# Counting the edges of a graph: from scattered additions to one-hot products on the matrix engine

## The reference

```
e   = leaky_relu(alpha_s[src] + alpha_d[dst]);  a = exp(e - max over dst) / sum over dst
out = segment_sum(h[src] * a, dst)                      # layer 0
agg = segment_sum(norm * (h[row] + edge_fea), col)      # layer 1, five times
```

## Time and profile before

| | us |
|---|---|
| runs of the kernel before | 4120.7, 4135.0, 4138.2 (median 4135.0) |
| span of the profiled execution | 4111.2 |
| attention loop, from first to last zz | 249 to 1694 of the span |
| busy: PE, DVE, POOL, ACT | 3273, 2226, 2136, 1341 |

### The profile page before, as it was taken

How to read it: one execution, slowest core, us unless ns; L and a number is a source line. 1 busy time by engine, 2 the same in 40 slices (tenths; PEclk the granted TensorE clock), 3 DMA queues, 4 the chain that set the end, 5 groups by cost and what they waited for, 6 DMA issues and landing times. The chain is left out here.

```text
span 4111.2 us, 65888 instructions
## 1 busy us (share of the span) xinstructions
PE 3273.1 (80%) x17046; PEld 2215.9 (54%) x17047; DVE 2226.4 (54%) x7140; ACT 1340.9 (33%) x3098; POOL 2136.4 (52%) x1893
## 2 busy tenths in 40 slices
PE   0758888888887878769999999996976777777778
PEld 0446666666655555546555555554455555555544
DVE  5657777777777777772222222225244445554468
ACT  3123333333333333232213131314553333433322
POOL 4366777777788888544454636310004545554510
PEclk9878898888989898879999999997998888888889
DMA  7468656656665556334444545342943323332320
GB/s 302 64 172 261 140 142 145 141 141 145 138 140 133 139 135 138 64 83 133 156 144 141 172 126 170 124 130 52 263 119 93 91 85 96 94 94 87 90 55 21
DMA packets 472113, 530.37 MB, mean 129 GB/s; under 512 B 192361, under 2 KB 376791, under 8 KB 471925
## 3 DMA queue, kind: packets, MB, share of 16 engines
q0 software_dynamic: 142496, 237.86, 24.0%
q1 hardware_dynamic: 316808, 271.48, 22.5%
q10 hardware_dynamic: 12749, 20.33, 1.4%
HBM read 438.46 MB, written 70.54 MB: 124 GB/s over the span
## 5 line engine op out<-in xcount | busy, mean ns | idle before, releaser
L1136 PE MATMUL p_out<-rows,hot 128*128 128x266 f32 x2048 | 665.4, 454 | 68.2 <-DVE rows L1273 53.5
L2217 POOL DMA_INDIRECT col_rows<-col_dram,m_idx x440 | 417.6, 949 | 473.1 <-ACT m_idx L2297 333.3
L1061 POOL DMA_INDIRECT count_dram<-number,place x348 | 587.9, 1689 | 144.9 <-issue 107.7
L1053 POOL DMA_INDIRECT rows<-att_dram,idx x512 | 526.1, 1028 | 216.7 <-issue 143.0
L1705 POOL DMA_INDIRECT rec_dram<-records,edge_place x416 | 407.8, 980 | 429.6 <-PE p_hi L1738 200.6
L1634 PE MATMUL p_lo<-cbuf,parts 128*128 128x400 f16 x1750 | 583.4, 333 | 5.1 <-issue 5.1
L1635 PE MATMUL p_hi<-cbuf,parts 128*128 128x400 f16 x1750 | 583.4, 333 | 4.0 <-issue 4.0
L1136 PEld LDWEIGHTS p_out<-rows,hot 128*128 128x128 f32 x2048 | 409.8, 222 | 170.1 <-DVE rows L1273 85.2
L1144 PE MATMUL p_out<-mask,ident_bf 128*128 128x240 bf16 x1788 | 361.4, 287 | 1.7 <-issue 1.7
L1273 DVE TENSOR_TENSOR rows<-rows 128x512 f32<-128x512 f32 x512 | 349.8, 684 | 0.2 <-issue 0.2
L1662 DVE TENSOR_TENSOR node_sum<-p_hi,low_sb 128x400 f32<-128x400 f32 x80 | 46.0, 574 | 557.5 <-ACT low_sb L1653 491.6
(11 more groups left out here) (421 smaller groups left out, 6126.7 us busy)
## 6 DMA issues: line engine op xcount, KB each, us to landing
cbuf<-count_dram SPq DMA_DIRECT2D x40, 2500.0 KB
dl_rep<-dl_dram SPq DMA_DIRECT2D x128, 256.0 KB
count_dram<-zeros SPq DMA_DIRECT2D x20, 1000.0 KB
g_rows<-count_dram SPq DMA_DIRECT2D x25, 800.0 KB, 4.7
rec_dram<-blank ACTq DMA_DIRECT2D x1, 17600.0 KB
m_group_rows<-rec_dram SPq DMA_DIRECT2D x110, 160.0 KB
records<-in_edges POOLq DMA_DIRECT2D x32, 520.0 KB
key_rep<-key_dram SPq DMA_DIRECT2D x64, 256.0 KB
```

The source lines that it names most:

```text
L1053: nc.gpsimd.indirect_dma_start(rows[r][:, u, :], None, att_dram, bass.IndirectOffsetOnAxis(ap=idx[r][:, u:u + 1].bitcast(U32), axis=0)).th ...
L1061: nc.gpsimd.indirect_dma_start(count_dram, bass.IndirectOffsetOnAxis(ap=place[r][:, n, c:c + 1].bitcast(U32), axis=0), number[r][:, 2 * n ...
L1136: m = nc.tensor.matmul(p_out[q][:, side, 0:HALF], hot[k][:, u, :], rows[k][:, u, side * HALF:(side + 1) * HALF], start=(u == 0), stop=(u = ...
L2217: nc.gpsimd.indirect_dma_start(col_rows[q][:, u, :], None, col_dram, bass.IndirectOffsetOnAxis(ap=idx[q][:, u:u + 1].bitcast(U32), axis=0) ...
```

## The change

The counts are made by PE. Destinations are cut in blocks ("windows") of WD = 10 nodes; for each the plan makes one or more count steps: (chunk of 128 edges, window). There are CT = 768 of them, CS = 6 per group of the attention loop. For a count step DVE makes two one-hot tables in bf16, `lo_hot` (edge by source modulo 128) and `key_hot` (edge by 25 source tiles times 10 destinations, 250 columns; -1 steps of other chunks match nothing), and PE multiplies them into a PSUM area `counts` of 3 banks; the table `step_table` says which window of the area a step belongs to. ACT copies the six windows (128 x 1500) to a 16-bit area `taken`, that lies over `x_sb`, once per group; SP stores it once per round (240 columns of 3200 rows, pieces of 480 bytes). A window that a group leaves open is taken into the next by `carry`.

```
 DVE, per group                                              # removed: alike x2/x4, if_first, at_place
+def count_hots(g, q, first, last):
+    for v in range(first, last):
+        TS(lo_hot[q][:, v, :], iota_bf[:], column(lo_step, g * CS + v), None, ALU.is_equal)
+        one = TS(key_hot[q][:, v, :], iota_key[:], column(key_step, g * CS + v), None, ALU.is_equal)
 PE, per group                                               # removed: keep_clock x7 (14 products)
             if within(j, 1):
                 turn_back(j + 1)
                 node_tops(j + 1, (k + 1) % 4)
+            at = (*read_registers(... j * CS, 1 ...), *read_registers(... j * CS + 1, CS - 1 ...))
+            add_up(j, k, 0)
+            add_up(j, k, 1)
+            clear(j)              # waits evacuated >= j; 3 products of 512 columns, fp16
+            if not is_first(j):
+                carry(at[0])      # 1 product of 250 columns
+            pe.wait_ge(hots_ready, j + 1)
+            for v in range(CS // 2): count(q, v, at[v])       # 250 columns each, bf16
+            add_up(j, k, 2)
+            for v in range(CS // 2, CS): count(q, v, at[v])
             if within(j, 2): turn(j + 2)
             if within(j, 1): look_up(j + 1, tiles[k])
             add_up(j, k, U - 1)
 ACT, per group, behind Exp(j) and ahead of take_scores(j + 2)
+def evacuate(b, n, r):
+    act.wait_ge(counted, n)
+    (at,) = read_registers(... take_table ...)
+    nc.scalar.copy(taken[:, :, bass.ds(at, CS * WD)]..., counts[:]...).then_inc(evacuated, 1)
 SP, once per round
+    sp.wait_ge(evacuated, i * 4); sp.wait_ge(stored, i * 16)
+    sp.dma_start(count_dram...[:, :, bass.ds(to, WIDE)], taken[:, :, bass.ds(side, WIDE)])
 POOL, per group                                             # removed: pair() x1/x2, place_ready wait
                 for u in range(U): gather((k + 3) % 4, u)
```

More of the change, by code:

```diff
@@ L893, in rounds @@
                 work(GROUPS - 4 + k, k, GROUPS // 4 - 1)
-        def rounds_in_two(engine, work):
-            for k in range(4):
-                work(k, k, 0, True)
-            for first, last, late in ((1, LATE_ROUNDS, True), (LATE_ROUNDS, GROUPS // 4 - 1, False)):
-                with engine.Fori(first, last) as i:
-                    for k in range(4):
-                        work(i * 4 + k, k, i, late)
-            for k in range(4):
-                work(GROUPS - 4 + k, k, GROUPS // 4 - 1, False)
-        def issued(k, i, late):
-            return i * (BODY - 2) + (PRE + (0, 4, 6, 8)[k]) if late else i * BODY + (PRE + PARTS[k][0] - 2 * LATE_ROUNDS)
         def within(j, ahead):
@@ L1055, in gather, with work @@
                                 bass.IndirectOffsetOnAxis(ap=idx[r][:, u:u + 1].bitcast(U32), axis=0)).then_inc(rows_in[r], 16)
-                        def pair(r, n, before):
-                            pool.wait_ge(placed, before * 16)
-                            pool.nop().then_inc(waits_passed, 1)
-                            for c in range(2):
-                                nc.gpsimd.indirect_dma_start(
-                                    count_dram, bass.IndirectOffsetOnAxis(ap=place[r][:, n, c:c + 1].bitcast(U32), axis=0),
-                                    number[r][:, 2 * n + c:2 * n + c + 1], None, compute_op=ALU.add).then_inc(placed, 16)
-                        def work(j, k, i, late):
-                            ahead = within(j, 3)
-                            r, before = (k + 3) % 4, issued(k, i, late)
-                            second = k == 0 or (k == 2 and not late)
-                            pool.wait_ge(place_ready, j + 1)
-                            if k % 2 == 0:
-                                pair(k, 0, before)
-                            if ahead:
+                        def work(j, k, i):
+                            if within(j, 3):
                                 pool.wait_ge(idx_ready, j + 4)
@@ L1076, in work @@
                                 pool.nop().then_inc(waits_passed, 1)
[L1077 to L1088 removed]
+                                for u in range(U):
+                                    gather((k + 3) % 4, u)
+                        nc.gpsimd.memset(nothing[:], 0.0).then_inc(empty_ready, 1)
                         for g in range(3):
@@ L1139, in add_up, with clear @@
                                 m.then_inc(sums_ready, 1)
-                        def keep_clock(k, n, fresh=False):
-                            for i in range(n):
-                                nc.tensor.matmul(p_out[k % 2][:, i % 2, 272:], ident_bf[:], mask[:, 1, 0:240], start=fresh, stop=True,
-                                                 skip_group_check=True)
+                        def clear(j):
+                            pe.wait_ge(empty_ready, 1 if is_first(j) else 2)
+                            if not is_first(j):
+                                pe.wait_ge(evacuated, j)
+                            for v in range(CS * AT // HALVES):
+                                nc.tensor.matmul(counts[:, v * HALVES:(v + 1) * HALVES], ident16[:], nothing[:], start=True, stop=False,
+                                                 skip_group_check=True)
@@ L1147, in work @@
                         def work(j, k, tiles):
-                            if not (isinstance(j, int) and j < 2):
-                                pe.wait_ge(added, j - 1)
-                            keep_clock(k, 2, True)
+                            q = k % 2
                             if within(j, 1):
                                 turn_back(j + 1)
-                                keep_clock(k, 2)
                                 node_tops(j + 1, (k + 1) % 4)
-                            for u in range(U - 1):
-                                keep_clock(k, 2)
-                                add_up(j, k, u)
+                            table = step_table[:].rearrange("o b i -> o (b i)")
@@ L1158, in work @@
+                            add_up(j, k, 2)
+                            for v in range(CS // 2, CS):
+                                m = count(q, v, at[v])
+                            m.then_inc(counted, 1)
                             if within(j, 2):
```

445 lines of the change are left out of this document (232 added, 213 removed).

## The result

The changed kernel is slower: 4259.8 us (median of 4 runs, 4239.1 to 4269.7) against 4133.9 (4120.7 to 4138.2), a ratio of 1.030 with a 95% interval of 1.027 to 1.034. The prediction was 3938, with a range of 3845 to 4055.

The account below looks back on a forecast made before the run. POOL's scatters were taken to bound the loop, then PE's chain. Terms -22 - 9 + 5 - 178 + 10 + 4 - 1 = -191 us took the 4111.2 span to 3920, forecast 3938 us, range 3845 to 4055.

Parts of the forecast that it names:

- POOL's scatters: Attention loop before: POOL's queue of gathers and scatters makes rows late; the loop loses 1.9 us per group to scatters.
- The chain of 9.66 us: Attention loop: PE's dependent steps of one group at full clock, 9.66 us, above DVE's 9.2, set the period.
- the fourth rival: Attention loop: without the fillers PE's clock falls and the kernel gets slower than before; 4318 us at f = 0.5, chance 0.06.
- 9.95 + 6 f: Loop period in us if a share f of groups runs at 1.2 GHz, where about 6 us of PE stream double.
- the floor: Loop period of 9.95 us per group: PE's chain of 9.66 plus 0.3 for DVE's table read.
- PE's register reads: Behind `node_tops`, six table values in two calls per group: taken at 0, at most 2.4 us.
- evacuation hidden: Attention loop: ACT's copy of 1500 columns, 1.9 us behind Exp, ends before PE reaches `clear`, so it costs nothing.
- single p_out free: Attention loop: `add_up(j, 0)` waiting for DVE to have added the previous sums costs nothing.
- third rival: Attention loop: stores of 480-byte pieces hold the DMA engines at 10.6 to 11.7 us a group; 4020 to 4160 us, chance 0.12.
- Ahead of the loop: Before the last barrier: no zero fill, early chunks or key work, less the new selection block; -26 at best, net -22 us.
- The barrier's -9: Last barrier ahead of the loop: without POOL's early scatters DVE goes on 9 us earlier.
- Behind the loop: After the last group: last evacuation and store +4 us (0 to 10), late scatters -1, reload of x hidden.

Follow-up runs that it names:

- e2: The kernel before with its 14 filler products per group left out (`keep_clock` returns at once); time +0.2%, period 11.12 us, clock 0.74.
- e7: The changed kernel with 14 fillers, constant places and the late three count products moved behind look_up; ratio moved within its interval against fillers and constants alone.
- e11: The changed kernel with 6 fillers in PE's waits, split early place reads and late counts behind look_up; 4034.6 us against 4113.6 before, ratio 0.980.
- e1: The changed kernel with the 14 filler products per group back at their old places; period 11.35 us, clock 0.96, 0.8% slower than before.
- e5: The changed kernel run again, unedited; 3967.4 us against 3827.2 before, period 12.22 us, clock 0.78.
- e3: The changed kernel with PE's count places as constants instead of register reads (wrong columns); loop 1427 us first to last zz, clock 0.81.
- e6: The changed kernel with 14 fillers and constant places together; loop 1349 us first to last zz, ratio to before 0.984.
- e18: e15 with PE's and DVE's node tiles also constants instead of table reads (sums land in wrong tiles); mean period 9.74 us.
- e15: The changed kernel with 6 fillers, late counts, constant places and small stores (one tile of 25); mean period 10.25 us.
- e14: e11 with constant places, so PE reads no register inside a group; mean period 10.40 us.
- e9: e8 with each store of the count matrix cut to one tile of 25 (128 pieces instead of 3200); period 10.61 us.
- e10: The changed kernel with 14 fillers, late counts behind look_up and one group's places read before the round's store; ratio to before 0.992.
- e12: The kernel before run again, unedited, beside the variants; 1440 us of loop, first zz at 248.8 us.
- e16: e8 run again, side by side with e17; period 11.27 us.
- e17: The small-store version e9 run again, side by side with e16; period 10.62 us.
- e4: The changed kernel with PE's two register reads moved ahead of the next group's turning product; ratio to before 1.029.
- e8: The changed kernel with 14 fillers, real places read ahead of the turning product and late counts behind look_up; period 11.66 us.
- e13: e11 with one group's places read behind the node products instead of the turning product; no gain that can be measured.

## Why the prediction was wrong

**What bounds before (POOL's scatters): right.** e2 makes PE slower (clock 0.74) at nearly the same time (+0.2%), and ACT waits for gathered rows as before.

**The chain of 9.66 us: the pieces were right at full clock.** In e7, at 0.99 and with no reads, a plain group gives

```profile
884.63 0.27 DVE L1321 TENSOR_TENSOR zz<-p_node,rows 128x64 f32<-128x64 f32 x1 [0.68 <-PE p_node L1145]
...
888.24 0.16 DVE L1258 TENSOR_SCALAR absent<-p_node 128x4 f32<-128x4 f32 x1
...
890.12 1.17 PE L1154 MATMUL p_out<-rows,hot 128*128 128x266 f32 x4 [0.40 <-DVE rows L1300]
...
894.73 0.26 DVE L1321 TENSOR_TENSOR zz<-p_node,rows 128x64 f32<-128x64 f32 x1 [0.28 <-PE p_node L1145]
```

3.61 + 1.88 + 4.61 against 3.27 + 1.93 + 4.46. The third piece of e7 has four fillers more and three count products less than the one predicted. The 1.49 us for 3286 new columns hold: in the kernel after, clear, carry and three counts take 1.09 us (1029.87 to 1030.96) and the other three 0.32. With 6 fillers (e11) the plain groups take 9.5. In the kernel after the same three pieces are 3.15 + 2.81 + 5.24 = 11.2: the second holds the read and a slow add_up 0, the third a slow add_up 1.

**The step that failed: the chain was taken "at full clock".** The prediction saw that "keepers ran while PE waited; most of the new products stand on the chain", and counted this as columns only. It is also what kept the clock. This was the fourth rival, at a chance of 0.06; its formula, 9.95 + 6 f with f = (1 - 0.77) / 0.5 = 0.46, gives 12.7 where 12.4 came. That it comes so close is luck: it puts 2.8 us on the clock and nothing on the reads. In the plain group above the eight slow products cost 8 x 0.22 = 1.8 us, and the fillers give back 0.87 us a group (e1 against e5). Its thresholds are off too: by its own sum the kernel is level with the one before at f = 197 / (127 x 6) = 0.26, not at 0.3. Of its two arguments against, "the new products fill the same time" contradicts the sentence quoted above, and "the long waits were POOL's doing" is refuted: in 400 to 1500 the kernel after waits 5.7 us for gathered rows and has a clock of 0.78, and e3, with 53.7 us of such waits and no reads inside a group, has 0.81. The Trainium skill ("TensorE: Matmul & The Clock Gate", HAM oscillation) says that PE's waits between bursts let the clock down and the next burst starts slow. The trace agrees, with add_up 0 and 1 behind the wait at 0.44 us a product and add_up 2 at 0.22. The prediction drew the wrong sign from it, because it took POOL's long waits for the cause and left the fillers out. What was missing is what holds the clock of before (the fillers: 0.89 with, 0.74 without) and what it is worth there (0.2%, e2).

The clock alone does not save the forecast: e1, at 0.96, is still 0.8% slower than before. Two more terms of the period were wrong, the reads and the floor. Of the 2.27 us by which e5's 12.22 lies above 9.95, fillers and constant places together take away 1.60 (e6), and 0.67 stays. So even with both mended the ratio is 0.984, where 3938 / 4135 is 0.952.

**PE's register reads, taken at 0 of a range of 0 to 2.4 us: 1.0 us** (period of e3 against e5), 0.7 with fillers (e6 against e1). The reads take 1.55 us behind node_tops, and PE's queue is in order, so the 0.8 us of slack that the prediction saw at add_up 0 could cover half of them at most; the read ends a median of 0.26 us before add_up 0. The Trainium skill ("Runtime: NRT & Kernel Launch", Instruction fetch mechanics) gives some 200 ns per register for register loads from HBM. Here the table lies in SBUF, and the records show somewhat more: 1.24 us for five values, 0.31 for one.

**The floor.** With clock and places mended (e6) the period is 10.6 over all groups, 10.4 in groups 8 to 119, against 9.95. The groups outside of 8 to 119, the first beside the fill of rec_dram, thus cost 23 us more, where 10 were put for the fill. DVE's table read, put at +0.3 a group (1.2 per round), measured 1.4 per round in e18 against e15; PE's, 0.9 per round, was left out of the sum. Eight of the 14 fillers stand on the chain: without them the plain groups fall from 10.1 to 9.5 (e11). These terms were not separated further.

**Right:** evacuation hidden (1.41 us for 1.9; in the group shown it ends at 1025.11 and `clear` starts at 1029.87); one-hots at 0.36 a pair for 0.40; single p_out free (in that group DVE has taken the sums at 1024.77, and add_up 0 starts at 1026.32); POOL at 35% of the loop, gathers no longer first among the waits.

**The store (third rival, 0.12).** No bound here: the DMA share is 0.70. A piece takes 59 ns on average in the last store (3200 pieces in some 10.5 us), against the 47 assumed; in the loop the mean is 66 to 79 ns in most stores and 28 to 34 in four. The store delays gathers in the quick versions, by some 0.15 us a group (e14, e15), and stretches register reads (e9).

**Ahead of the loop: -4 for -26 in the first pair of traces, some -13 and -20 in others** (e10 against e12, e5 against e2). The 25 equal DVE instructions were to lose their gaps with the zero fill. In the first pair they keep part of them without it (25.4 us from first to last start, 33.6 before), and in e2 they have none with it (50.3 to 64.2, DMA share 1.02 in 50 to 78). After and e2:

```profile
L633 DVE SCALAR_TENSOR_TENSOR in_tile<-src_tile,iota_row,every x25: 641/652/692, 39.7 to 65.1; 128x416 bf16<-128x416 f32 x25
```

```profile
L656 DVE SCALAR_TENSOR_TENSOR in_tile<-src_tile,iota_row,every x25: 636/641/682, 50.3 to 64.2; 128x416 bf16<-128x416 f32 x25
```

In the sessions in which before takes 3824 to 3835 us no kernel has gaps there, with the fill or without. In the others they add up to 17 and 18 us with it (e12, before) and to 4 to 20 without it, 20 and 7 in e16 and e17, which ran side by side. So they come without the fill too; whether it adds to them, and what makes them, is open. The node table's products start 2.5 us earlier in the first pair and 11 to 14 in two others (148.2 to 136.9 in e12 and e10, 139.8 to 125.5 in e2 and e1).

The barrier's -9 did come, and more: from the last product of the node table to DVE's first instruction behind the barrier it is 20.6 us before and 9.2 after, and DVE's wait there falls from 12.54 us to 1.13. It was lost again at once. From there to the first zz it is 20.2 us before and 30.1 after, where +5 stood for storing and clearing x. ACT waits 9.26 us for the first gathered rows while the store of x is under way, and then POOL clears `x_sb`:

```profile
214.88 0.88 DVE L1221 TENSOR_TENSOR tab<-acc,tab 128x400 f32<-128x400 f32 x1 [1.13 <-PEq L164]
231.11 0.30 ACT L1014 COPY scores<-rows 128x64 f32<-128x64 f32 x1 [9.26 <-DMA rows<-att_dram,idx]
232.26 5.44 POOL L1109 MEMSET x_sb<- 128x6400 f32 x1 [1.78 <-DMA x_dram<-x_sb]
233.25 4.47 DVE L1240 TENSOR_SCALAR rhs<-last_step 128x4 f32<-128x4 f32 x1 [0.78 <-PE p_step L1126]
237.78 1.89 PE L1135 MATMUL p_node<-rhs,hot 128*128 128x17 f32 x8 [4.57 <-DVE rhs L1241]
```

DVE's L1240 takes a median of 0.17 us over the loop; here it takes 4.47 us and ends at 237.72, as POOL's MEMSET does (237.70), and PE waits for it. It is so in every traced kernel that clears `x_sb` (3.9 to 5.3 us). The other increase, the late first rows, was not taken apart.

**Behind the loop: +13 for +3.** The end of the kernel after:

```profile
1827.49 1.41 ACT L1050 CAST x_sb<-counts 128x1500 f32 x1 [6.77 <-PE counts L1171]
...
1830.21 0.41 SPq L993 DMA_DIRECT2D count_dram<-x_sb  x1
...
1843.54 0.35 SPq L1003 DMA_DIRECT2D x_sb<-x_dram  x1
```

The last store alone takes 13.3 us from its issue to the next instruction of SP, all of it ahead of the barrier. The prediction had put 4 us (0 to 10) for the evacuation of 1.9 us and the 1.5 MB together; its packets alone take 10.5 us (1831.2 to 1841.7).

**Open:** what makes the gaps between the 25 instructions, and the 230 us of layer 3 between sessions; and what lengthens single groups of k0 and k2 in e18.

## What to carry to other kernels

A filler product, or any other work that only occupies an engine's waits, is a part of the design: before it is counted as columns saved, ask which products follow its place, and price these at the lower clock too. When a bound engine is freed, everything that its lateness had hidden (a slow clock, a read in an in-order queue) comes onto the path at once, so the ceiling of the gain has to be read from a group in which all of that already counts. Register reads (here 0.25 to 0.31 us a value) are paid in the in-order queue where they stand: put them behind work long enough to cover them, and away from a burst of small stores.

## What the runs showed of the hardware

- PE's read of five values from an SBUF table takes 1.24 us (one value 0.31), and a median of 3.8 to 4.4 us while a store of 3200 pieces of 480 bytes has the DMA engines at a share of 1.04; with 128 pieces it is 1.24 (e4, e8, e16 against e9, e17).
- In a loop of 11.2 us per group in which PE waits 0.8 us for DVE ahead of the node products, the granted clock was 0.81 and half of the add_up products ran at 1.2 GHz (e3). Six fillers of 240 columns per group gave 0.93 to 0.96 (e11, e13 to e15, e18), fourteen 0.93 to 0.99 (e1, e6 to e10, e16, e17), none 0.74 to 0.81 (e2 to e5).
- While POOL's MEMSET of 128 x 6400 values ran (5.44 us), a DVE instruction of 128 x 4 values that takes 0.17 us otherwise took 4.47 us and ended with it (after; 3.9 to 5.3 us in the other 16 traces with this MEMSET).
- The same program differed by 7% between sessions (before: 3824 to 3835 us in some, 4113 to 4134 in others), most of it in layer 3 (some 230 us). The number of the chip does not tell which it will be: the results name chip 6 for 3835 and for 4113, and chip 10 for 4114 and for 3824. The loop moves less: the changed kernel's took 1573 us in one session and 1553 in another.
